# Column sums from chunks that GpSimd added before, and a correction whose two parts share one matmul

## The chip, the cores and the metric

The kernel runs on one core of one Trainium2 chip. Its engines work at the same time and meet through semaphores: TensorE (PE) for matmuls, with its weight loads shown apart as PEld, VectorE (DVE), ScalarE (ACT), GpSimd (POOL), and SyncE (SP), which issues the DMAs. The metric is the device time of one execution in microseconds (us), median of several runs.

## The reference, cut to what matters

A decoder layer for 2 x 256 tokens of width 512: self-attention with 32 heads, then a product with a context in fake-quantised numbers, then a linear layer with low-rank experts. The change touches the second of the three.

```python
def fake_quant(x, scale, zp):
    s = scale.reshape(()); z = zp.reshape(())
    q = jnp.clip(jnp.round(x / s + z), 0.0, 255.0)
    return (q - z) * s

def _L0_xattn_ref(x1, x2, x1_scale, x1_zp, x2_scale, x2_zp):
    return jnp.matmul(fake_quant(x1, x1_scale, x1_zp), fake_quant(x2, x2_scale, x2_zp))

x = x + attn(layernorm(x), Wq, bq, Wk, bk, Wv, bv, Wo, bo, gq, gk)
x = x + _L0_xattn_ref(layernorm(x), ctx_4096, ...)     # ctx: (2, 512, 512)
x = x + ffn(layernorm(x), ...)
```

## The kernel before, in words

The 512 tokens are four tiles of 128 partitions (t = 0 to 3, two for each batch). Projections, scores and products of the attention are done in float32 split into a high and a low part (`_hi`, `_lo`, three matmuls for each product); ScalarE makes the high part, VectorE or GpSimd subtracts it to make the low part.

**Order of the work.** Every engine has its own list of instructions, written out by hand, and executes it in that order; semaphores hold it where it needs another engine. First all heads of K and Q are projected. Then come 16 pairs of heads (`pair(p)`, p = 0 to 14, and `last_pair`). A pair has four slots (j = 0 to 3), one for each head and batch. In a slot TensorE does the scores of the *next* slot (L602 to L604), the transposes of the normalised probabilities (L611), a quarter of the V projection of the next pair (L625 to L627), the output projection of the previous head (L639 to L641) and probabilities times V (L670 to L672).

**GpSimd in a pair** (L1086): in slots 0 and 2 it makes the low parts of k and q for the next head (`split_kq_lo`, L1070 and L1072), then the low part of a piece of the V weights (`w_lo`, L1062); in slots 1 and 3 the low part of the output weights (`wo_lo`, L1062). TensorE waits for k_lo and q_lo (semaphore `kq_lo`) before the scores in slots 1 and 3. SP waits for GpSimd's weight parts (`w_lo_pool`) before it loads the next weights into the same place.

**VectorE in a slot**: maximum of the scores (`nmax`, L1293), its product with the row scale (`nbias`, L1295), which ScalarE needs for the exponentials (L858), the low part of the probabilities (L1368), and, after the exponentials, the reciprocal of the sum (L1300) and the two halves of the normalisation (L1302 and L1303), which TensorE needs for the transposes (semaphore `p_normed`).

**The quantised product.** Codes of context and activations are kept with 128 taken off, as small whole numbers. So the product of real values needs two corrections: one for each row (made later, `row_sums`), and one for each column, the sum of the context's codes down its 512 rows times a constant. The context is quantised early, waits in HBM as bf16 and comes back as `ctx_q` (4 chunks of 128 rows for each batch) at 413 us. For each batch `column_sums` multiplies a matrix of ones with the four chunks (L421), ScalarE scales the sums into `corr_hi` (L880), VectorE makes the remainder `corr_lo` (L1431), and `add_column_part` adds both to each token tile in `acc[t]` by multiplying with the identity (L429, L430). `column_sums(0)` stands in slot 3 of the last pair, `column_sums(1)` behind it, `add_column_part` behind the attention.

Of the kernel before, what the change touches and what calls it, by code (L numbers as in the profile page):

```python
# [19 lines left out]
F32 = mybir.dt.float32  # L20
F32R = mybir.dt.float32r
BF16 = mybir.dt.bfloat16
I32 = mybir.dt.int32
ALU = mybir.AluOpType
ACT = mybir.ActivationFunctionType
AX = mybir.AxisListType

P = 128
B, S, D = 2, 256, 512
T = B * S  # L30
NT = T // P
NC = D // P
SKV = 512
NH, DH = 32, 128
NP = NH // 2
# [14 lines left out]
def decoder_layer(nc, x, ctx_t, wk, wq, wv, wo, bk, bq, bv, bo, gk, gq, qscal, ra_w, base_b, router_b, bm_w,  # L50
                  expert_map, out):
    st = ExitStack()
    with st:
        def sem(name):
            return st.enter_context(nc.semaphore(name))
# [18 lines left out]
        def here(name, shape, dt, at=None):  # L74
            return place(name, shape, dt, at)[0]
# [4 lines left out]
        q_all, q_at = place("q_all", [P, NH, T], F32)  # L80
# [17 lines left out]
        ident_r = here("ident_r", [P, P], F32R)  # L98
# [19 lines left out]
        qc = here("qc", [P, 8], F32)  # L118
# [3 lines left out]
        half = NT * PW * 4  # L122
# [8 lines left out]
        KS = T * 4  # L131
# [20 lines left out]
        ctx_q = here("ctx_q", [P, B * NC, SKV], BF16, k_at + 18 * KS)  # L152
        xn = here("xn", [P, NT, D], F32, q_at)
        q1t = here("q1t", [P, NT, NC, P], BF16, q_at + 6 * KS)
        corr_hi = here("corr_hi", [P, B, SKV], F32R, q_at + 8 * KS)
        corr_lo = here("corr_lo", [P, B, SKV], F32R, q_at + 4 * KS)
        hw = here("hw", [P, NT, P], F32, q_at + 10 * KS)
        ones_b = here("ones_b", [P, P], BF16, q_at + 11 * KS)
        small_at = q_at + 12 * KS
        emf = here("emf", [P, NR], F32, small_at)  # L160
        onehot = here("onehot", [P, NE, NR], F32, small_at + 128)
# [26 lines left out]
        acc = [bank(f"acc{t}", [P, D]) for t in range(NT)]  # L188
# [4 lines left out]
        p_flat = [p_v[:].rearrange("p a b -> p (a b)"), p_s[:].rearrange("p a b -> p (a b)"),  # L193
                  p_t[:].rearrange("p a b -> p (a b)"), p_o[:]]
# [50 lines left out]
        ctx_back = sem("ctx_back")  # L245
# [15 lines left out]
        wo_last_done = sem("wo_last_done")  # L261
        x1_ready = sem("x1_ready")
        ones_b_made = sem("ones_b_made")
        ctx_quantised = sem("ctx_quantised")
        col_sums_ready = sem("col_sums_ready")
        col_part_done = sem("col_part_done")
# [41 lines left out]
        def peeled(n, first, end):  # L308

            return isinstance(n, int) and first <= n < end  # L310
# [104 lines left out]
        def column_sums(pe, b):  # L415

            if b == 0:
                pe.wait_ge(ctx_back, 16)
                pe.wait_ge(ones_b_made, 1)
            for c in range(NC):  # L420
                mm = pe.matmul(p_flat[b], ones_b[:], ctx_q[:, b * NC + c, :], start=(c == 0), stop=(c == NC - 1))  # L421
            mm.then_inc(col_sums_ready, 1)

        def add_column_part(pe, t):

            if t % 2 == 0:
                pe.wait_ge(col_lo_done, t // 2 + 1)
            pe.wait_ge(linear_done, t + 1)
            pe.matmul(acc[t][:], ident_r[:], corr_hi[:, t // 2, :], start=False, stop=False, skip_group_check=True)  # L429
            pe.matmul(acc[t][:], ident_r[:], corr_lo[:, t // 2, :], start=False, stop=True, skip_group_check=True  # L430
                      ).then_inc(col_part_added, 1)

        def transpose_q1(pe, t):
# [341 lines left out]
        def _(act):  # L775
# [101 lines left out]
            def column_part(b):  # L877

                act.wait_ge(col_sums_ready, b + 1)
                act.activation(corr_hi[:, b, :], p_flat[b], ACT.Copy, scale=qc[:, 3:4]  # L880
                               ).then_inc(col_part_done, 1)

            def last_out_hi(n):
# [140 lines left out]
        def _(pool):  # L1024
# [52 lines left out]
            def mark_experts():  # L1077
# [5 lines left out]
                    ins = pool.tensor_scalar(onehot[:, e, :], emf[:], float(e), None, ALU.is_equal)  # L1083
                ins.then_inc(experts_marked, 1)

            def pair(p, par):  # L1086
                for j in range(4):
                    h = 2 * p + j // 2
                    if j % 2 == 0:
                        split_kq_lo(h + 1)  # L1090
                        pair_chunk_lo(par, j // 2, 0, 4 + 4 * p + j)
                    else:
                        chunk_lo(wo_lo[:], wo_hi[:], 1, 4 + 4 * p + j)
                    if peeled(p, NP - 5, NP - 4) and j == 0:
                        pool.memset(ones_b[:], 1.0).then_inc(ones_b_made, 1)

            def last_pair():
                n = 4 + 4 * (NP - 1)
# [28 lines left out]
        def _(dve):  # L1127
# [79 lines left out]
            for r in range(1, 4):  # L1207
# [4 lines left out]
                                          op0=ALU.mult, op1=ALU.mult))  # L1212
# [215 lines left out]
            def column_lo(b):  # L1428

                dve.wait_ge(col_part_done, b + 1)  # L1430
                dve.scalar_tensor_tensor(out=corr_lo[:, b, :], in0=p_flat[b], scalar=qc[:, 3:4],  # L1431
                                         in1=corr_hi[:, b, :], op0=ALU.mult, op1=ALU.subtract
                                         ).then_inc(col_lo_done, 1)

            def row_part():
# [101 lines left out]
            for t in range(NT):  # L1537
# [5 lines left out]
                                          op0=ALU.is_lt, op1=ALU.mult))  # L1543
# [6 lines left out]
            for t in range(NT):  # L1550

                ins = dve.scalar_tensor_tensor(out=hw[:, t, :].rearrange("p (e r) -> p e r", e=NE),
                                               in0=acc[t][:, 0:P].rearrange("p (e r) -> p e r", e=NE), scalar=2.0,
                                               in1=gate[:, t, :].unsqueeze(2).to_broadcast([P, NE, RK]),
                                               op0=ALU.mult, op1=ALU.mult)
# [4 lines left out]
            for n, (t, cols, y) in enumerate(out_parts()):  # L1560
# [3 lines left out]
                                         in1=x_res[:, t, cols], op0=ALU.add, op1=ALU.add).then_inc(out_done, 1)  # L1564
# [54 lines left out]
```

## Time and profile before

| | us |
|---|---|
| median of 3 runs (533.52 to 533.87) | 533.6 |
| span of the profiled execution, first to last instruction | 531.9 |
| what lies around the span (533.6 less 531.9; the profiled execution's own time is not listed apart) | 1.7 |
| TensorE busy, share of the span | 520.5, 98% |
| VectorE busy | 332.6, 63% |
| ScalarE busy | 354.6, 67% |
| GpSimd busy | 264.4, 50% |

The granted TensorE clock is 1.000 over the span, the higher of its two levels (2.4 GHz). Matmuls are pipelined and their ends are modelled, so for TensorE the step from one start to the next counts, not the duration of one. The times in the rows further down are microseconds from the span's start. In that count the attention's pairs run from about 194 to 492 us, a pair takes 18.8 us and a slot 4.7 us.

### The profile page before, as it was taken

How to read it: one execution, taken by the hardware profiler on the slowest of the kernel's cores; microseconds unless marked ns; L12 is line 12 of the kernel's file. 1: busy time of each engine (PE TensorE's matmuls, PEld its weight loads, DVE VectorE, ACT ScalarE, POOL GpSimd, SP SyncE). 2: the span in 40 equal slices, each digit the busy share in tenths (PEclk: the TensorE clock that was granted, in tenths of full speed). 3: DMA queues.
4: the chain of work that ended last, by engine and by line, in shares of the span. 5: the costliest groups of instructions: out<-in, count | busy, mean ns of one | idle time of the engine just before them, and what ended most of it. 6: DMA issues, size and time to landing. Idle time of an engine off the chain costs nothing.

```text
span 531.9 us, 9795 instructions
## 1 busy us (share of the span) xinstructions
PE 520.5 (98%) x3221; PEld 462.3 (87%) x3221; DVE 332.6 (63%) x703; ACT 354.6 (67%) x743; POOL 264.4 (50%) x223
## 2 busy tenths in 40 slices
PE   7999999999999999999999999999999999999897
PEld 6888888878888888999999999999999999997586
DVE  6354444276666677666766666666666677766855
ACT  4666665656666767767767776777767777766730
POOL 2444444364455545564646556465564646542340
PEclk9999999999999999999999999999999999999999
DMA  5445635323333221122121122211132322121002
GB/s 184 139 139 166 209 99 163 95 79 99 99 99 95 63 82 51 51 59 60 59 59 52 47 59 59 59 59 55 46 124 77 138 61 60 42 58 41 1 1 80
DMA packets 23495, 43.43 MB, mean 82 GB/s; under 512 B 3632, under 2 KB 3888, under 8 KB 23216
## 3 DMA queue, kind: packets, MB, share of 16 engines
q1 hardware_dynamic: 23472, 43.13, 27.0%
q8 instruction: 13, 0.21, 0.2%
q14 instruction: 10, 0.08, 0.1%
HBM read 41.03 MB, written 2.10 MB: 81 GB/s over the span
## 4 chain that ended last, share of the span: by engine, by line
PE 90%; DVE 5%; ACT 2%; DMA 1%; POOL 1%; issue 0%; SPq 0%; DVEq 0%; ACTq 0%
PE p_v L627 5%; PE p_v L625 5%; PE p_o L548 5%; PE p_o L549 5%; PE p_o L550 5%; PE p_v L626 5%; PE p_t L548 5%; PE p_t L550 5%; PE p_t L549 5%; PE acc L639 5%; PE acc L640 5%; PE p_t L611 5%; PE acc L641 5%; PE p_o L670 3%; PE p_o L672 3%; PE p_o L671 3%
## 5 line engine op out<-in xcount | busy, mean ns | idle before, releaser
L1193 DVE TENSOR_TENSOR w_lo<-raw,w_hi 128x512 fp32r<-128x512 f32 x64 | 44.2, 690 | 77.0 <-ACT w_hi L782 77.0
L1062 POOL TENSOR_TENSOR wo_lo<-raw,wo_hi 128x512 fp32r<-128x512 f32 x31 | 40.2, 1297 | 100.7 <-ACT wo_hi L936 97.2
L858 ACT ACTIVATE probs<-p_s,nbias,rq_t 128x256 f32<-128x256 f32 x128 | 71.3, 562 | 19.4 <-DVE nbias L1295 19.4
L782 ACT CAST w_hi<-raw 128x512 fp32r<-128x512 f32 x64 | 39.9, 623 | 62.7 <-PE p_t L550 30.3
L625 PE MATMUL p_v<-w_hi,xnt_hi 128*128 128x256 f32 x256 | 77.2, 302 | 0.0
L627 PE MATMUL p_v<-w_hi,xnt_lo 128*128 128x256 f32 x256 | 72.3, 283 | 0.0
L626 PE MATMUL p_v<-w_lo,xnt_hi 128*128 128x256 f32 x256 | 72.2, 282 | 0.0
L1044 POOL TENSOR_TENSOR acc_k<-acc_k,square 128x512 f32<-128x512 f32 x32 | 41.6, 1301 | 52.7 <-ACT square L797 52.7
L1044 POOL TENSOR_TENSOR acc_q<-acc_q,square 128x512 f32<-128x512 f32 x32 | 43.5, 1360 | 40.2 <-ACT square L797 39.9
L912 ACT CAST pt_hi<-p_t 128x512 fp32r<-128x512 f32 x64 | 37.4, 584 | 37.6 <-PE p_t L611 37.6
L1062 POOL TENSOR_TENSOR w_lo<-raw,w_hi 128x512 fp32r<-128x512 f32 x32 | 44.8, 1400 | 23.4 <-ACT w_hi L842 23.4
L1293 DVE TENSOR_REDUCE nmax<-p_s 128x2 f32<-128x512 f32 x64 | 43.9, 686 | 13.4 <-PE p_s L604 12.5
L548 PE MATMUL p_o<-xnt_hi,w_hi 128*128 128x512 f32 x128 | 49.8, 389 | 0.0
L549 PE MATMUL p_o<-xnt_hi,w_lo 128*128 128x512 f32 x128 | 49.8, 389 | 0.0
L550 PE MATMUL p_o<-xnt_lo,w_hi 128*128 128x512 f32 x128 | 49.8, 389 | 0.0
L625 PEld LDWEIGHTS p_v<-w_hi,xnt_hi 128*128 128x128 f32 x256 | 48.8, 191 | 0.3 <-issue 0.2
L626 PEld LDWEIGHTS p_v<-w_lo,xnt_hi 128*128 128x128 f32 x256 | 48.9, 191 | 0.0
L548 PE MATMUL p_t<-xnt_hi,w_hi 128*128 128x512 f32 x124 | 48.8, 393 | 0.0
L627 PEld LDWEIGHTS p_v<-w_hi,xnt_lo 128*128 128x128 f32 x256 | 48.7, 190 | 0.0
L550 PE MATMUL p_t<-xnt_lo,w_hi 128*128 128x512 f32 x124 | 48.3, 389 | 0.0
L549 PE MATMUL p_t<-xnt_hi,w_lo 128*128 128x512 f32 x124 | 48.3, 389 | 0.0
L639 PE MATMUL acc<-wo_hi,o_hi 128*128 128x512 f32 x120 | 47.6, 397 | 0.1
(287 smaller groups left out, 1486.7 us busy)
## 6 DMA issues: line engine op xcount, KB each, us to landing
raw<-in_wv SPq DMA_DIRECT2D x36, 256.0 KB, 2.6
raw<-in_wk SPq DMA_DIRECT2D x32, 256.0 KB, 2.6
raw<-in_wq SPq DMA_DIRECT2D x32, 256.0 KB, 2.6
raw<-in_wo SPq DMA_DIRECT2D x31, 256.0 KB, 2.6
ctx_f<-in_ctx SPq DMA_DIRECT2D x4, 512.0 KB, 3.7
xin<-in_x SPq DMA_DIRECT2D x4, 256.0 KB, 3.4
xb<-in_x SPq DMA_DIRECT2D x4, 256.0 KB, 5.6
ctx_kept<-ctx_k SPq DMA_DIRECT2D x1, 1024.0 KB, 5.0
```

Of the source, the lines that this page charges most:

```text
L548: pe.matmul(p_flat[2 + n], hi[:, c, :], xnt_hi[:, c, :], start=(c == 0), stop=False)
L549: pe.matmul(p_flat[2 + n], lo[:, c, :], xnt_hi[:, c, :], start=False, stop=False)
L550: mm = pe.matmul(p_flat[2 + n], hi[:, c, :], xnt_lo[:, c, :], start=False, stop=(c == NC - 1))
L625: pe.matmul(p_v[:, t % 2, :], xnt_hi[:, c, tt], hi[:, c, :], start=(c == 0), stop=False)
L626: pe.matmul(p_v[:, t % 2, :], xnt_hi[:, c, tt], lo[:, c, :], start=False, stop=False)
L627: mm = pe.matmul(p_v[:, t % 2, :], xnt_lo[:, c, tt], hi[:, c, :], start=False, stop=(c == NC - 1))
L639: pe.matmul(acc[t][:], o_hi[:, tt], wo_hi[:], start=False, stop=False, skip_group_check=True)
L858: act.activation(probs[:, n, a, :], p_s[:, a, :], ACT.Exp, bias=nbias[:, n, a:a + 1], scale=rq_t[:, 2 * b + a:2 * b + a + 1], accum_out=rs ...
L1044: pool.tensor_tensor(sums[:], sums[:], square[:, r % 2, :], ALU.add).then_inc(summed, 1)
L1062: pool.tensor_tensor(dst, raw[:, slot, :], hi, ALU.subtract).then_inc(w_lo_pool, 1)
L1193: dve.tensor_tensor(w_lo[:, n, 0:NC * DH], raw[:, r, :], w_hi[:, n, 0:NC * DH], ALU.subtract).then_inc(w_lo_dve, 1)
L1293: dve.tensor_reduce(nmax[:, n, :], p_s[:], AX.X, ALU.max, negate=True).then_inc(max_done, 1)
```

## The change

GpSimd adds the four chunks of each batch's context codes, with three additions of 128x512 for each batch, in slots 1, 2 and 3 of the pairs 13 and 14 (`add_ctx`). The sum is float32 (`ctx_sum`), and `column_sums` is one matmul for each batch in place of four. The correction's high part is written to all 128 partitions of `corr`, and VectorE then overwrites partitions 64 to 127 with the low part. All rows of each half are alike, so a matrix `two_rows` with ones in rows 0 and 64 and zeros elsewhere adds one row of each: one matmul for each token tile in place of two. GpSimd makes the new constants in pair 11.

```diff
-        corr_hi = here("corr_hi", [P, B, SKV], F32R, q_at + 8 * KS)
-        corr_lo = here("corr_lo", [P, B, SKV], F32R, q_at + 4 * KS)
+        ctx_sum = here("ctx_sum", [P, B, SKV], F32R, q_at + 8 * KS)
+        corr = here("corr", [P, B, SKV], F32R, q_at + 4 * KS)
...
+        ones_r = here("ones_r", [P, P], F32R, q_at + 11 * KS + 512)
+        two_rows = here("two_rows", [P, P], F32R, q_at + 11 * KS + 1024)
...
         def column_sums(pe, b):
             if b == 0:
-                pe.wait_ge(ctx_back, 16)
-                pe.wait_ge(ones_b_made, 1)
-            for c in range(NC):
-                mm = pe.matmul(p_flat[b], ones_b[:], ctx_q[:, b * NC + c, :], start=(c == 0), stop=(c == NC - 1))
-            mm.then_inc(col_sums_ready, 1)
+                pe.wait_ge(ones_b_made, 4)
+            pe.wait_ge(ctx_summed, (NC - 1) * (b + 1))
+            pe.matmul(p_flat[b], ones_r[:], ctx_sum[:, b, :], start=True, stop=True).then_inc(col_sums_ready, 1)
...
             pe.wait_ge(linear_done, t + 1)
-            pe.matmul(acc[t][:], ident_r[:], corr_hi[:, t // 2, :], start=False, stop=False, skip_group_check=True)
-            pe.matmul(acc[t][:], ident_r[:], corr_lo[:, t // 2, :], start=False, stop=True, skip_group_check=True
+            pe.matmul(acc[t][:], two_rows[:], corr[:, t // 2, :], start=False, stop=True, skip_group_check=True
                       ).then_inc(col_part_added, 1)
...
-                act.activation(corr_hi[:, b, :], p_flat[b], ACT.Copy, scale=qc[:, 3:4]
+                act.activation(corr[:, b, :], p_flat[b], ACT.Copy, scale=qc[:, 3:4]
                                ).then_inc(col_part_done, 1)
...
+            def add_ctx(b, c):
+                if c == 1:
+                    pool.wait_ge(ctx_back, 16)
+                    first = ctx_q[:, b * NC, :]
+                else:
+                    pool.wait_ge(ctx_summed, (NC - 1) * b + c - 1)
+                    first = ctx_sum[:, b, :]
+                pool.tensor_tensor(ctx_sum[:, b, :], first, ctx_q[:, b * NC + c, :], ALU.add).then_inc(ctx_summed, 1)
+
             def pair(p, par):
                 for j in range(4):
...
                     if peeled(p, NP - 5, NP - 4) and j == 0:
                         pool.memset(ones_b[:], 1.0).then_inc(ones_b_made, 1)
+                        pool.memset(ones_r[:].bitcast(F32), 1.0).then_inc(ones_b_made, 1)
+                        pool.memset(two_rows[:].bitcast(F32), 0.0).then_inc(rows_cleared, 1)
+                        pool.wait_ge(rows_cleared, 1)
+                        pool.memset(two_rows[0:1, :].bitcast(F32), 1.0).then_inc(ones_b_made, 1)
+                        pool.wait_ge(ones_b_made, 3)
+                        pool.memset(two_rows[P // 2:P // 2 + 1, :].bitcast(F32), 1.0).then_inc(ones_b_made, 1)
+                        pool.wait_ge(ones_b_made, 4)
+                    if peeled(p, NP - 3, NP - 1) and j > 0:
+                        add_ctx(p - (NP - 3), j)
...
-                dve.scalar_tensor_tensor(out=corr_lo[:, b, :], in0=p_flat[b], scalar=qc[:, 3:4],
-                                         in1=corr_hi[:, b, :], op0=ALU.mult, op1=ALU.subtract
+                half = slice(P // 2, P)
+                dve.scalar_tensor_tensor(out=corr[half, b, :], in0=p_flat[b][half], scalar=qc[half, 3:4],
+                                         in1=corr[half, b, :], op0=ALU.mult, op1=ALU.subtract
                                          ).then_inc(col_lo_done, 1)
```

GpSimd's list in the kernel before, from slot 1 of pair 13 to slot 1 of pair 14. `kq_hi` and `w_hi_done` are ScalarE's semaphores for high parts.

```order
L1062 TENSOR_TENSOR wo_lo<-raw,wo_hi 128x512 [waits w_hi_done]
L1070 TENSOR_TENSOR k_lo<-k_all,k_hi 128x512 [waits kq_hi]
L1072 TENSOR_TENSOR q_lo<-q_all,q_hi 128x512 [waits kq_hi]
L1062 TENSOR_TENSOR w_lo<-raw,w_hi 128x512 [waits w_hi_done]
L1062 TENSOR_TENSOR wo_lo<-raw,wo_hi 128x512 [waits w_hi_done]
L1070 TENSOR_TENSOR k_lo<-k_all,k_hi 128x512 [waits kq_hi]
L1072 TENSOR_TENSOR q_lo<-q_all,q_hi 128x512 [waits kq_hi]
L1062 TENSOR_TENSOR w_lo<-raw,w_hi 128x512 [waits w_hi_done]
L1062 TENSOR_TENSOR wo_lo<-raw,wo_hi 128x512 [waits w_hi_done]
```

The same stretch in the changed kernel; L1095 is the new addition.

```order
L1063 TENSOR_TENSOR wo_lo<-raw,wo_hi 128x512 [waits w_hi_done]
L1095 TENSOR_TENSOR ctx_sum<-ctx_q 128x512 [waits ctx_back]
L1071 TENSOR_TENSOR k_lo<-k_all,k_hi 128x512 [waits kq_hi]
L1073 TENSOR_TENSOR q_lo<-q_all,q_hi 128x512 [waits kq_hi]
L1063 TENSOR_TENSOR w_lo<-raw,w_hi 128x512 [waits w_hi_done]
L1095 TENSOR_TENSOR ctx_sum<-ctx_sum,ctx_q 128x512 [waits ctx_summed]
L1063 TENSOR_TENSOR wo_lo<-raw,wo_hi 128x512 [waits w_hi_done]
L1095 TENSOR_TENSOR ctx_sum<-ctx_sum,ctx_q 128x512 [waits ctx_summed]
L1071 TENSOR_TENSOR k_lo<-k_all,k_hi 128x512 [waits kq_hi]
L1073 TENSOR_TENSOR q_lo<-q_all,q_hi 128x512 [waits kq_hi]
L1063 TENSOR_TENSOR w_lo<-raw,w_hi 128x512 [waits w_hi_done]
L1063 TENSOR_TENSOR wo_lo<-raw,wo_hi 128x512 [waits w_hi_done]
```

Nothing of the old list has changed its order, but the additions of slots 1 and 3 stand in front of k_lo and q_lo, and that of slot 2 stands between w_lo and wo_lo. Pair 14 has the same three, and the last of them has no k_lo behind it, since head 31 is split elsewhere.

TensorE's list in the kernel before, from the last slot of the attention to the first correction. `q1_done` is VectorE's semaphore for quantised activations, `linear_done` ScalarE's for the step ahead of it.

```order
L421 MATMUL p_s<-ctx_q,ones_b 128x512 x4
L657 MATMUL acc<-wo_last_hi,o_last_hi 128x512 [waits wo_last_done,o_lo_done]
L658 MATMUL acc<-wo_last_hi,o_last_lo 128x512
L659 MATMUL acc<-wo_last_lo,o_last_hi 128x512
L657 MATMUL acc<-wo_last_hi,o_last_hi 128x512
L658 MATMUL acc<-wo_last_hi,o_last_lo 128x512
L659 MATMUL acc<-wo_last_lo,o_last_hi 128x512
L439 MATMUL p_t<-ident,xn 128x128 [waits q1_done]
L439 MATMUL p_t<-ident,xn 128x128 x3
L429 MATMUL acc<-corr_hi,ident_r 128x512 [waits linear_done,col_lo_done]
L430 MATMUL acc<-corr_lo,ident_r 128x512
L429 MATMUL acc<-corr_hi,ident_r 128x512 [waits linear_done]
```

And in the changed kernel:

```order
L424 MATMUL p_s<-ctx_sum,ones_r 128x512 [waits ctx_summed]
L658 MATMUL acc<-wo_last_hi,o_last_hi 128x512 [waits wo_last_done,o_lo_done]
L659 MATMUL acc<-wo_last_hi,o_last_lo 128x512
L660 MATMUL acc<-wo_last_lo,o_last_hi 128x512
L658 MATMUL acc<-wo_last_hi,o_last_hi 128x512
L659 MATMUL acc<-wo_last_hi,o_last_lo 128x512
L660 MATMUL acc<-wo_last_lo,o_last_hi 128x512
L440 MATMUL p_t<-ident,xn 128x128 [waits q1_done]
L440 MATMUL p_t<-ident,xn 128x128 x3
L431 MATMUL acc<-corr,two_rows 128x512 [waits linear_done,col_lo_done]
L431 MATMUL acc<-corr,two_rows 128x512 [waits linear_done]
```

Six matmuls of the column sums and four of the correction are gone; the rest keeps its order, and so do VectorE's and ScalarE's lists.

## Rows read from the trace of the kernel before

**Rows 1.** The page, part 4: shares of the chain that ended last.

```profile
PE 90%; DVE 5%; ACT 2%; DMA 1%; POOL 1%; issue 0%; SPq 0%; DVEq 0%; ACTq 0%
```

**Rows 2.** Busy time by stretch: the stretch, its length, each engine's busy time.

```profile
448.48:457.87 9.39, 9.39 (x71) 8.85 (x70) 6.75 (x16) 7.12 (x18) 5.29 (x4) 1.00 0.20 56
```

**Rows 3.** GpSimd in order of time: start, length, operation, idle before and releaser.

```profile
448.84 1.33 POOL L1062 TENSOR_TENSOR wo_lo<-raw,wo_hi 128x512 fp32r<-128x512 f32 x1 [3.25 <-ACT wo_hi L936]
450.45 1.30 POOL L1070 TENSOR_TENSOR k_lo<-k_all,k_hi 128x512 fp32r<-128x512 f32 x1 [0.29 <-ACT k_hi L845]
451.71 1.29 POOL L1072 TENSOR_TENSOR q_lo<-q_all,q_hi 128x512 fp32r<-128x512 f32 x1
453.59 1.42 POOL L1062 TENSOR_TENSOR w_lo<-raw,w_hi 128x512 fp32r<-128x512 f32 x1 [0.59 <-ACT w_hi L842]
...
458.23 1.33 POOL L1062 TENSOR_TENSOR wo_lo<-raw,wo_hi 128x512 fp32r<-128x512 f32 x1 [3.22 <-ACT wo_hi L936]
...
461.10 1.30 POOL L1072 TENSOR_TENSOR q_lo<-q_all,q_hi 128x512 fp32r<-128x512 f32 x1
...
467.62 1.32 POOL L1062 TENSOR_TENSOR wo_lo<-raw,wo_hi 128x512 fp32r<-128x512 f32 x1 [3.23 <-ACT wo_hi L936]
...
470.25 1.30 POOL L1072 TENSOR_TENSOR q_lo<-q_all,q_hi 128x512 fp32r<-128x512 f32 x1
```

**Rows 4.** TensorE's weight loads in order of time: first scores of slots, a transpose.

```profile
453.18 0.19 PEld L602 LDWEIGHTS p_s<-k_hi,q_hi 128*128 128x128 f32 x1
...
453.92 0.14 PEld L611 LDWEIGHTS p_t<-ident,probs 128*128 128x128 f32 x1
...
462.57 0.19 PEld L602 LDWEIGHTS p_s<-k_hi,q_hi 128*128 128x128 f32 x1
...
471.95 0.19 PEld L602 LDWEIGHTS p_s<-k_hi,q_hi 128*128 128x128 f32 x1
```

**Rows 5.** VectorE in order of time, slot 2 of pair 13.

```profile
451.28 0.49 DVE L1295 TENSOR_TENSOR nbias<-nmax,rq_t 128x2 f32<-128x2 f32 x1
...
453.24 0.36 DVE L1302 TENSOR_SCALAR probs<-probs,rinv 128x256 f32<-128x256 f32 x1
453.51 0.35 DVE L1303 TENSOR_SCALAR probs<-probs,rinv 128x256 f32<-128x256 f32 x1
```

**Rows 6.** VectorE and GpSimd in order of time, where they meet at 113 us.

```profile
112.96 0.69 DVE L1193 TENSOR_TENSOR w_lo<-raw,w_hi 128x512 fp32r<-128x512 f32 x1
...
113.24 1.56 POOL L1044 TENSOR_TENSOR acc_q<-acc_q,square 128x512 f32<-128x512 f32 x1 [1.12 <-ACT square L797]
...
113.57 1.78 DVE L1198 SCALAR_TENSOR_TENSOR k_all<-k_all,g_c,rkb 128x512 f32<-128x512 f32 x1
```

**Rows 7.** The chain that ended last, in order of time: start, length, work.

```profile
475.62 0.24 PE acc L641
...
477.95 2.79 DMA raw<-in_wo
...
490.75 0.86 PE p_v L421 x4
...
497.56 0.23 PE acc L430
```

**Rows 8.** VectorE, ScalarE and TensorE in order of time, behind the attention.

```profile
493.09 0.74 DVE L1431 SCALAR_TENSOR_TENSOR corr_lo<-p_v,qc,corr_hi 128x512 fp32r<-128x512 f32 x1
494.26 0.48 DVE L1344 SCALAR_TENSOR_TENSOR o_last_lo<-p_o,bv_c,o_last_hi 128x256 fp32r<-128x256 f32 x1 [0.42 <-ACT o_last_hi L888]
...
497.36 0.69 ACT L983 ACTIVATE q1t<-p_t,qc 128x512 bf16<-128x512 f32 x1 [0.54 <-PE p_t L439]
...
498.11 0.39 PE L450 MATMUL p_v<-ctx_q,q1t 128*128 128x512 bf16 x1
...
502.61 0.42 DVE L1419 TENSOR_SCALAR xn<-xn 128x512 f32<-128x512 f32 x1
...
503.08 0.65 PE L439 MATMUL p_o<-ident,xn 128*128 128x128 f32 x4
```

More of the change, by code:

```diff
@@ L263, in decoder_layer @@
         ones_b_made = sem("ones_b_made")
+        rows_cleared = sem("rows_cleared")
+        ctx_summed = sem("ctx_summed")
         ctx_quantised = sem("ctx_quantised")
```

## The prediction

> **What bounds the kernel now.** I read the page first. Its chain of the work that ended last lies on TensorE for 90% [rows 1]: a stall of TensorE costs its own length unless something slower runs beside it. Then the busy times by stretch: two slots of pair 13 and 14, 9.39 us, are filled by TensorE without a gap, GpSimd is busy for 5.29 us of them [rows 2]. So GpSimd has 4.1 us free in two slots, but the average does not say where. The engine's own rows do [rows 3]: its free time lies in front of wo_lo (3.25 us) and in front of w_lo (0.59 us); wo_lo, k_lo and q_lo follow each other with hardly a gap (448.84, 450.45, 451.71). q_lo ends at 451.71 + 1.29 = 453.00, and the scores that wait for it start on TensorE at 453.18 [rows 4]. These 0.18 us are the number on which the forecast rests. Last I read the chain in order of time around 475 us and behind the attention [rows 7], and VectorE's rows there [rows 8].
>
> **What the change removes.** Ten matmuls of 128x512. The four bf16 ones of a column sum take 0.86 us on the chain, 0.215 each; a correction matmul takes 0.23 [rows 7]. That is 6 x 0.215 + 4 x 0.23 = 2.2 us of TensorE time at most, if all of it were on the path. The one that stays of each four now has fp32r inputs; the correction's own matmuls have them too and take 0.23, so I price it at that.
> The Trainium skill (FP8 and Floating Point Precision, TensorE Precision Notes) has true FP32 matmuls make four passes through the array, while its reduced-precision reading does not. Were the four-pass rule the one for this matmul, the column sums would save nothing; the 0.23 us of the row is one pass, so the trace sides with the reduced reading.
>
> How much of the 2.2 us is on the path:
> - Column sum 0 is in front of the last output projections. Its three matmuls, 0.65 us, let the last p_o end earlier. But o_last_lo, which follows p_o, stands on VectorE behind corr_lo, which does not move: it ends at 493.09 + 0.74 = 493.83, and o_last_lo started at 494.26 [rows 8]. With the next instruction following about 0.07 us before the end of the one ahead, o_last_lo comes at 493.78: 0.5 us gained, the rest lost in this wait. Everything up to the first quantised tile hangs on it.
> - Column sum 1 runs while TensorE would wait for o_last_lo anyway: 0. It only lets ScalarE's column part come early enough for the 0.5 to pass on.
> - Corrections of tiles 0 and 1: the product behind them needs q1t, which ends at 497.36 + 0.69 = 498.05; it started at 498.11 [rows 8]. 0 to 0.06, I take 0.
> - Corrections of tiles 2 and 3: the transposes behind them started at 503.08, 0.05 after VectorE's quantisation ended at 502.61 + 0.42 = 503.03 [rows 8]. 0.
> VectorE's remainder on half the partitions has as many elements in each partition; I give it the old 0.74. Gain in all: 0.5 us. Bounds: 0, and the 2.2 us.
>
> **What it adds: first stall, the scores.** No row shows GpSimd adding bf16. The nearest are its 128x512 fp32 instructions with two inputs: 1.29 to 1.56 us long [rows 3, 6], and 451.71 - 450.45 = 1.26 from start to start. I take 1.28 and, as bounds, 0.5 (no row is near it) and 1.6. Three of the six additions stand in front of k_lo and q_lo:
> - Pair 13, slot 1. wo_lo starts at 448.84, so the addition at 450.12, k_lo at 451.40 in place of 450.45, and q_lo ends at 453.95 in place of 453.00. The scores start on TensorE about 0.06 behind it, at 454.01 in place of 453.18: 0.83 us.
> - Pair 13, slot 3. wo_lo 458.23, addition 459.51, k_lo 460.77, q_lo 462.03 to 463.33 in place of 461.10 to 462.40; scores 463.39 in place of 462.57: 0.82.
> - Pair 14, slot 1. wo_lo 467.62, addition 468.90, k_lo 470.16, q_lo 471.42 to 472.72; scores 472.78 in place of 471.95: 0.83. Here 0.40 us lay between the old q_lo and the scores, but GpSimd had no gap to give.
> Together 2.5 us. In a formula each is the addition's time less 0.45.
>
> **Second stall, the normalisation.** The same late q_lo covers VectorE's normalisation. In the rows nbias, a 128x2 product of two tiles in SBUF, takes 0.49 us from 451.28, to 451.77, just behind the end of k_lo at 451.75 [rows 3, 5]: VectorE was held until GpSimd's instruction ended. The halves of the normalisation (453.24 and 453.51) escaped this, because q_lo was over at 453.00 and w_lo came at 453.59, and its 1.42 us instead of 1.29 say that w_lo waited for the second half instead. Now: nbias waits for the addition only (to 451.47), the exponentials and with them the first half come 0.3 earlier, at 452.93, but q_lo runs from 452.66 to 453.95. The first half gets in at its end. w_lo, whose high part is ready, stands right behind. At 113.24 a GpSimd instruction was waiting when VectorE's at 112.96 ended, and the next of VectorE, at 113.57, took 1.78 us: the waiting GpSimd instruction went first [rows 6]. By this the second half waits for w_lo, which ends at 453.90 + 1.38 = 455.3, and is done at 455.4. The transposes, which started at 453.92 [rows 4], start at 455.45: 1.53 us late, 0.83 of it already counted. So 0.7 us more; the other two places, with the same distances, give 0.7 each. Together 2.1 us. Bounds: 0 (the second half slips in before w_lo) and 1.0 each (the first half is held too).
> The Trainium skill (SBUF — State Buffer, Who interferes with whom) says that VectorE's two-port modes and GpSimd exclude each other for a whole instruction, and that the order of issue decides who waits. By issue order w_lo (453.90) is ahead of the second half (454.02), which gives the same 0.7; but this margin of 0.1 us is what makes the second stall less sure than the first.
>
> **What stays at nothing.** The additions behind w_lo (slot 2) lie in the 3.2 us in front of wo_lo [rows 3]; 1.28 us fit even with w_lo 1.7 late, as TensorE's own delay moves wo_lo by 1.5. They may hold one nbias, inside that same delay. The last addition (pair 14, slot 3) comes behind the last wo_lo that starts the 2.79 us weight transfer on the chain [rows 7], and can hold VectorE only beside it: 0, at most 0.2. If that cover were gone it would cost one addition. SP's weight loads wait for w_lo, 1.7 late, but the copy of those weights comes two slots later. The memsets in pair 11 fall into the same kind of 3.2 us gap. The new wait of TensorE for the sums is over 10 us old when it gets there.
>
> **Does a stall come back?** The chain leaves TensorE at 475.62, with the output projection that frees wo_hi, and goes on over wo_lo and the transfer [rows 7]. All three places are earlier, and TensorE has no idle time between them and there that could be used up. So all of it counts.
>
> **Sum.** +2.5 + 2.1 - 0.5 = +4.1 us on the profiled 531.9 us of span, 536.0; with the 1.7 us around the span 537.7, which is also the median 533.6 + 4.1.
>
> **The rivals.**
> 1. *Only the scores stall.* The second half of the normalisation slips in. For it: the margin of 0.1 us, and that no normalisation in the trace was ever held. Against it: 113 us. 533.6 + 2.5 - 0.5 = 535.6. If it slips in at some of the three places, 536.3 or 537.0.
> 2. *A longer addition.* The bf16 input or the mixed types cost GpSimd more, 1.6 us: three times 0.3 more, 538.6. Nothing in the trace speaks for or against.
> 3. *Faster: the additions are short.* If two bytes an element make them cheap, the stalls of 3 x (a - 0.45) fall under the gain of 0.5 once an addition a takes less than 0.62 us, and the normalisation is then not covered. At 0.45 us or less the time is 533.6 - 0.5 = 533.1. Against it: every GpSimd instruction with 512 elements and two inputs in the rows takes twice that.
> 4. *No change.* Stalls of the scores for a short addition of 0.6 us against the gain: 533.6.
>
> **Chances.** Forecast 50%, the first rival with its mixed cases 31%, the second 9%, the third 5%, the fourth 5%. About 0.2%, 1.1 us, is what a measurement of this kernel can tell from no change. Faster 0.04, same 0.06, slower 0.90. The range takes in the first two rivals and the bounds around them and leaves out the third and fourth: 534.8 to 539.0.
>
> **What will show it.** Right: the scores' first weight load in slots 1 and 3 shows idle time of 0.7 to 0.9 us released by GpSimd's q_lo, three times, and nowhere else; L1303's longest row grows from 0.35 to over 1 us three times, and the transposes wait for it; behind the attention the first quantised tile comes 0.5 us sooner relative to the end of the last slot. The first step is wrong if GpSimd's additions last under 0.6 us or TensorE shows no idle there. The second is wrong if L1303 stays at 0.35. The gain is wrong if the stretch from the last transposes of the attention to the end shrinks by more than 0.7 us or not at all.

## The result

| | before | after |
|---|---|---|
| median, same chip (4 runs each) | 533.72 | 536.53 (536.49 to 536.88) |
| span of the profiled execution | 531.9 | 535.0 |

The ratio is 1.0053 (95% interval 1.0039 to 1.0066): the change costs 2.8 us. The forecast was 4.1 (537.7), the range 534.8 to 539.0. The direction held. The two stalls of the forecast came together at one of its three places; at the other two a third one, which it did not name, stood instead. That the range holds 536.5 is in part luck.

I set the weight loads of both traces side by side, instruction by instruction, and noted where the distance grows. It is 0.52 us after the first microseconds (the input's transposes, before anything that changed; the profiled run is the longest of its four), stays so for 440 us, and then:

| place, time after | distance | TensorE waits for |
|---|---|---|
| pair 13 slot 1, 453.7 | 0.52 to 1.28 | pt_lo |
| pair 13 slot 3, 463.9 | 1.28 to 2.02 | pt_lo |
| pair 14 slot 1, 474.6 and 476.1 | 2.02 to 3.38 | q_lo, then probs |
| pair 14 slot 3, 483.1 | to 3.54 | |
| weight transfer, 486.5 | to 3.15 | |
| column sums, 494.0 | to 2.54 | |
| o_last_lo, and up to 506.1 | 2.90, 3.07 | |

Three places cost 0.76 + 0.74 + 1.36 = 2.86 us. The last addition (pair 14 slot 3) costs 0.16 us more, beside the weight transfer. Behind the attention 0.5 to 0.6 us is won (3.15 to 2.54) and nearly all lost again (3.07 at the end). Some 0.2 of the step at the transfer belongs to the profiled run of before: the kernel of e13_waits_only below, with the work of before, shows 0.2 there too. The other 0.2 is about what the last addition had cost.

### The profile page after: what moved, and what is told of

It is laid out like the page before. It is cut to its first block, busy times and chain, and to the rows that moved or that the text cites. A ratio compares the mean times of both kernels' runs of the same rounds, so it can differ in the third digit from the quotient of the medians.

```text
span 535.0 us, 9785 instructions
## 1 busy us (share of the span) xinstructions
PE 520.3 (97%) x3210; PEld 461.7 (86%) x3211; DVE 336.2 (63%) x703; ACT 354.3 (66%) x743; POOL 271.5 (51%) x233
## 4 chain that ended last, share of the span: by engine, by line
PE 86%; DVE 7%; ACT 3%; DMA 1%; POOL 1%; issue 1%; SPq 0%; DVEq 0%; ACTq 0%
PE p_o L549 5%; PE p_o L551 5%; PE p_o L550 5%; PE p_t L549 5%; PE p_t L551 5%; PE p_t L550 5%; PE p_v L626 5%; PE p_v L628 5%; PE p_v L627 5%; PE acc L640 5%; PE acc L641 5%; PE p_t L612 5%; PE acc L642 5%; PE p_o L671 3%; PE p_o L673 3%; PE p_o L672 2%
```

## The profile after

The page, part 4, answers to [rows 1]; TensorE's share is 4% lower than before:

```profile
PE 86%; DVE 7%; ACT 3%; DMA 1%; POOL 1%; issue 1%; SPq 0%; DVEq 0%; ACTq 0%
```

The third place first, since there both stalls of the forecast are seen. GpSimd, VectorE and TensorE's weight loads in order of time, pair 14 slot 1; they answer to [rows 3, 4]:

```profile
469.64 1.32 POOL L1063 TENSOR_TENSOR wo_lo<-raw,wo_hi 128x512 fp32r<-128x512 f32 x1 [3.24 <-ACT wo_hi L937]
470.93 1.16 POOL L1095 TENSOR_TENSOR ctx_sum<-ctx_q 128x512 fp32r<-128x512 bf16 x1
472.05 1.28 POOL L1071 TENSOR_TENSOR k_lo<-k_all,k_hi 128x512 fp32r<-128x512 f32 x1
473.31 1.27 POOL L1073 TENSOR_TENSOR q_lo<-q_all,q_hi 128x512 fp32r<-128x512 f32 x1
474.55 1.32 POOL L1063 TENSOR_TENSOR w_lo<-raw,w_hi 128x512 fp32r<-128x512 f32 x1
...
471.71 0.40 DVE L1315 TENSOR_TENSOR nbias<-nmax,rq_t 128x2 f32<-128x2 f32 x1
...
473.58 1.15 DVE L1322 TENSOR_SCALAR probs<-probs,rinv 128x256 f32<-128x256 f32 x1
474.65 1.36 DVE L1323 TENSOR_SCALAR probs<-probs,rinv 128x256 f32<-128x256 f32 x1
...
474.63 0.19 PEld L603 LDWEIGHTS p_s<-k_hi,q_hi 128*128 128x128 f32 x1 [0.58 <-POOL q_lo L1073]
...
476.07 0.20 PEld L612 LDWEIGHTS p_t<-ident,probs 128*128 128x128 f32 x2 [0.66 <-DVE probs L1323]
```

The scores wait for q_lo. The two halves of the normalisation, 0.35 us of work each, take 1.15 and 1.36: the first is held until q_lo ends (474.58), and w_lo, which starts there, goes ahead of the second.

The first place went another way. The same engines, pair 13 slot 1; nbias and probs answer to [rows 5]:

```profile
449.36 1.31 POOL L1063 TENSOR_TENSOR wo_lo<-raw,wo_hi 128x512 fp32r<-128x512 f32 x1 [3.23 <-ACT wo_hi L937]
450.62 1.16 POOL L1095 TENSOR_TENSOR ctx_sum<-ctx_q 128x512 fp32r<-128x512 bf16 x1
451.75 1.29 POOL L1071 TENSOR_TENSOR k_lo<-k_all,k_hi 128x512 fp32r<-128x512 f32 x1
453.00 1.27 POOL L1073 TENSOR_TENSOR q_lo<-q_all,q_hi 128x512 fp32r<-128x512 f32 x1
...
451.80 1.25 DVE L1315 TENSOR_TENSOR nbias<-nmax,rq_t 128x2 f32<-128x2 f32 x1
452.98 0.68 DVE L1388 TENSOR_TENSOR pt_lo<-p_t,pt_hi 128x512 fp32r<-128x512 f32 x1
...
454.52 0.35 DVE L1322 TENSOR_SCALAR probs<-probs,rinv 128x256 f32<-128x256 f32 x1
454.79 0.35 DVE L1323 TENSOR_SCALAR probs<-probs,rinv 128x256 f32<-128x256 f32 x1
...
453.71 0.19 PEld L671 LDWEIGHTS p_o<-pt_hi,v_hi 128*128 128x128 f32 x1 [0.88 <-DVE pt_lo L1388]
...
454.41 0.19 PEld L603 LDWEIGHTS p_s<-k_hi,q_hi 128*128 128x128 f32 x1
```

The addition ends at 450.62 + 1.16 = 451.78 and k_lo starts at 451.75. nbias, 0.16 us of work when free, starts at 451.80, 0.05 behind k_lo, and is held until k_lo ends at 453.04. VectorE works in order, so pt_lo is late and TensorE waits for it, 0.88 us (0.76 of it new), ahead of the scores. That wait hides the late q_lo (454.27, scores 454.41), and the exponentials come so late that the normalisation meets no q_lo. At the second place the same: k_lo 461.87, nbias 461.90 and 1.28 long.

Behind the attention, VectorE in order of time, against [rows 8]. The first row is of before, the others of the changed kernel (`vare` is the variance that the layer norm needs next):

```profile
493.02 0.17 DVE L1405 TENSOR_SCALAR vare<-mv 128x2 f32<-128x2 f32 x1
...
496.17 0.17 DVE L1425 TENSOR_SCALAR vare<-mv 128x2 f32<-128x2 f32 x1
496.37 0.76 DVE L1452 SCALAR_TENSOR_TENSOR corr<-p_v,qc,corr 64x512 fp32r<-64x512 f32 x1
497.16 0.48 DVE L1364 SCALAR_TENSOR_TENSOR o_last_lo<-p_o,bv_c,o_last_hi 128x256 fp32r<-128x256 f32 x1
```

corr starts 0.20 after vare's start, where corr_lo stood 0.07 after it in the trace of before, and o_last_lo starts only when corr has ended (497.13), not 0.07 ahead of its end.

## The experiments

**e1_adds_only.** The kernel before with the six additions (`add_ctx`) where the changed kernel has them, and nothing else of the change; the sums go unused.

```
+        ctx_sum = here("ctx_sum", [P, B, SKV], F32R, q_at)
...
+                    if peeled(p, NP - 3, NP - 1) and j > 0:
+                        add_ctx(p - (NP - 3), j)
```

> The kernel before with the six GpSimd additions in their new places, and nothing else of the change: column sums and corrections stay as before, the additions' result is not used. Theory (the additions alone make the kernel slower, through places 1 to 3 in front of k_lo and q_lo): the same three stalls of TensorE as in the changed kernel, 0.8, 0.75 and 1.35 us, 0.2 of it won back at the weight transfer, so +2.7 us, 536.4. Rival (part of the 2.8 us comes from the new matmuls or the new wait for the sums): clearly under +2.7, 535.5 or less.

Measured: 536.55 us (536.31 to 536.73), before 533.86, ratio 1.0052 (1.0039 to 1.0066). The loss comes from the additions. The changed kernel lost 2.8 us on its before and this one 2.7, so the matmuls that fell away gave nothing that these runs can tell. nbias was 1.28, 1.26 and 0.39 us long at the three places, as in the changed kernel.

**e4_longer.** The two additions ahead of k_lo in pair 13 take 576 columns instead of 512 (the 64 more land where the second batch's sums are written later). They last 1.30 us.

```
+                if b == 0 and c != 2:
+                    n = SKV + 64
...
+                    pool.tensor_tensor(sums[:, 0:n], first, flat[:, c * SKV:c * SKV + n], ALU.add)
```

> The changed kernel with the two additions of pair 13 that stand in front of k_lo 64 columns longer, 576 in place of 512 (the surplus is overwritten later). Theory (what is lost hangs on which GpSimd instruction nbias meets): the additions last 0.13 us longer, 1.29 in place of 1.16, end behind the moment nbias is issued, and nbias slips in at their end, in place of missing it by 0.02 us and waiting out k_lo. Then these two places turn into what pair 14 shows, scores late by about 0.75 us and transposes by 0.65 more: +1.3 us, 537.8. Rival (each addition costs its length): 2 x 0.13 = +0.26 us, 536.8.

Measured: 538.15 us (537.3 to 538.46), ratio 1.0083 (1.007 to 1.0097). VectorE and TensorE at the first place:

```profile
450.94 0.16 DVE L1323 TENSOR_TENSOR nbias<-nmax,rq_t 128x2 f32<-128x2 f32 x1
...
452.57 1.15 DVE L1330 TENSOR_SCALAR probs<-probs,rinv 128x256 f32<-128x256 f32 x1
453.64 1.37 DVE L1331 TENSOR_SCALAR probs<-probs,rinv 128x256 f32<-128x256 f32 x1
...
453.63 0.19 PEld L603 LDWEIGHTS p_s<-k_hi,q_hi 128*128 128x128 f32 x1 [0.73 <-POOL q_lo L1073]
...
455.06 0.20 PEld L612 LDWEIGHTS p_t<-ident,probs 128*128 128x128 f32 x2 [0.67 <-DVE probs L1331]
```

0.14 us more on an addition moves k_lo past nbias, and both stalls of the forecast are there, 0.73 + 0.67 us; the second place shows the same two waits, 0.73 and 0.67. With additions of about the length that I had assumed (1.28) in pair 13, the loss is 4.3 us on this before (533.86), beside the 4.1 of the forecast. It is 0.35 more than I had expected of this run; its trace, of the shortest of the five runs, shows 1.4 us more at the three places than the changed kernel.

**e5_behind_q.** The three additions stand behind q_lo instead of ahead of k_lo.

> The changed kernel with the three additions that stood in front of k_lo now behind q_lo, in front of w_lo. Theory (the shared port alone costs): k_lo and q_lo are on time, but the addition holds the first half of the normalisation until it ends, w_lo goes ahead of the second half, and the transposes come 1.5 us late at three places: +4.5 us on the kernel before, 538.2. If w_lo does not go ahead of the second half: 0.5 us a place, 535.1. Rival (what costs is that k_lo and q_lo are late): nothing is late for TensorE, 533.6.

Measured: 538.22 us (537.9 to 538.6), ratio 1.0085 (1.0071 to 1.0098). Pair 13:

```profile
453.24 1.17 POOL L1095 TENSOR_TENSOR ctx_sum<-ctx_q 128x512 fp32r<-128x512 bf16 x1
454.36 1.31 POOL L1063 TENSOR_TENSOR w_lo<-raw,w_hi 128x512 fp32r<-128x512 f32 x1
...
453.51 1.04 DVE L1328 TENSOR_SCALAR probs<-probs,rinv 128x256 f32<-128x256 f32 x1
454.48 1.35 DVE L1329 TENSOR_SCALAR probs<-probs,rinv 128x256 f32<-128x256 f32 x1
...
455.88 0.20 PEld L612 LDWEIGHTS p_t<-ident,probs 128*128 128x128 f32 x2 [1.64 <-DVE probs L1329]
```

No score waits here; the held normalisation alone makes TensorE wait 1.6, 1.6 and 1.4 us at the three places. So holding the normalisation costs by itself, without a late k_lo or q_lo. The first half is held by the addition, the second by w_lo: one GpSimd instruction each.

**e2_gaps.** The additions stand behind w_lo, in slots 0 and 2 of pairs 12 to 14, where GpSimd is idle for 3.2 us.

```
-                    if peeled(p, NP - 3, NP - 1) and j > 0:
-                        add_ctx(p - (NP - 3), j)
+                    if peeled(p, NP - 4, NP - 1) and j % 2 == 0:
+                        n = 2 * (p - (NP - 4)) + j // 2
+                        add_ctx(n // 3, n % 3 + 1)
```

> The changed kernel with each addition behind w_lo, in slots 0 and 2 of pairs 12, 13 and 14, where GpSimd has 3.2 us free, none in front of k_lo. Theory (only the place of the additions costs): no stall of TensorE at scores, probabilities or transposes; the tail keeps its gain of 0.1 to 0.26 us; 533.5, that is 0.2 us under the kernel before and 3.0 under the changed one. Rival (GpSimd's additions cost wherever they stand, through the port that VectorE shares with it): six additions cost about 0.4 us each, 536.

Measured: 535.02 us (533.69 to 536.44, 7 runs), before 533.86, ratio 1.0024 (1.0011 to 1.0037): neither value. Its trace has one new cause of stalls, in pair 13 (0.5 us of TensorE, then 1.0):

```profile
445.70 1.16 POOL L1095 TENSOR_TENSOR ctx_sum<-ctx_sum,ctx_q 128x512 fp32r<-128x512 f32 x1
...
445.70 1.18 DVE L1316 TENSOR_TENSOR nbias<-nmax,rq_t 128x2 f32<-128x2 f32 x1
...
449.48 1.55 DVE L1379 TENSOR_TENSOR bm_lo<-bm_f,bm_hi 128x512 fp32r<-128x512 f32 x1
...
452.32 1.12 DVE L1316 TENSOR_TENSOR nbias<-nmax,rq_t 128x2 f32<-128x2 f32 x1
...
454.10 0.19 PEld L671 LDWEIGHTS p_o<-pt_hi,v_hi 128*128 128x128 f32 x1 [1.12 <-DVE pt_lo L1389]
```

nbias and the addition start in the same moment and nbias is held. That makes VectorE 1 us late, its next instruction with two SBUF inputs (bm_lo) meets wo_lo, and the next nbias meets q_lo. At 426.90 and 465.97 the two also started together, and there nbias lasted 0.16. A coin, it seemed, which would explain a spread of 2.7 us over 7 runs. A later nbias (475.35, 0.96 long, 0.23 behind the start of an addition) is held too and costs TensorE nothing.

**e6_low_first, e8_gated, e9_gated_low.** The first is the changed kernel with the low part on partitions 0 to 63. The others are e2_gaps with a gate meant to settle the coin, and with both edits.

```
 e6, e9:
-                half = slice(P // 2, P)
+                half = slice(0, P // 2)
 e8, e9, ahead of add_ctx:
+                        pool.wait_ge(nb_done, 4 * p + j + 2)
```

> The changed kernel with one slice turned round: VectorE writes the low part on partitions 0 to 63 instead of 64 to 127 (the high part then stands on 64 to 127; the sum over the two rows is the same). In the changed kernel corr lasts 0.76 us and begins 0.20 after vare, and o_last_lo begins only when it ends. Theory: VectorE's instructions on the upper half wait for the pipeline on either side, about 0.12 us twice. Then on the lower half corr begins 0.07 after vare, o_last_lo 0.07 before corr's end, and the matmul part of the gain is whole: 0.2 to 0.25 us less than the changed kernel, 536.3 beside its 536.5. Rival: the two gaps come from the semaphore wait on ScalarE's corr or from reading p_flat and corr with fewer partitions; then nothing moves, 536.5.

> The whole change, with the six additions behind w_lo in slots 0 and 2 of pairs 12 to 14, and ahead of each a wait of GpSimd for that slot's nbias. In the run with the additions in those slots and no such wait, nbias and the addition started at the same moment three times; nbias was held once (445.70, 1.18 us, the ungated run cost 1.2 us over the kernel before), and not at 426.90 (0.16). Theory: the only cost in these slots is that coincidence, and an addition that starts after nbias ends before the two scalings of probs 1.4 us later. Then no nbias and no probs is held in these slots, TensorE has no new idle time up to the tail, and the tail's gain of 0.26 stands alone: 533.6 beside a kernel before of 533.86 (533.4 to 533.8). Rival A: the additions still hold the scalings of probs or late_lo (bm_lo), 534.5 or more. Rival B: GpSimd's shared access slows others in a way that no held instruction shows, and the additions cost 0.1 to 0.2 each wherever they stand: 534.5.

> The additions waiting for nbias in slots 0 and 2 of pairs 12 to 14, and the low part on partitions 0 to 63: both corrections at once. By both theories the tail's gain is 0.45 to 0.5 us and nothing else is lost: 533.4 beside a kernel before of 533.86, ratio 0.999, the only version expected to beat the kernel before. Rival: the gain in the tail is taken back by GpSimd's later work there (onehot and rstd end later in the changed kernel by 0.15 us), 533.6, no difference that can be told.

Measured: e6 536.0 us (535.89 to 536.91), ratio 1.0042 (1.0029 to 1.0055); e8 534.24 (533.88 to 535.95, 12 runs), 1.0015 (1.0005 to 1.0025); e9 535.08 (533.06 to 536.85, 12 runs), 1.0019 (1.0004 to 1.0033); before 533.78.

In e6 the tail behaves as on full partitions again:

```profile
496.65 0.17 DVE L1425 TENSOR_SCALAR vare<-mv 128x2 f32<-128x2 f32 x1
496.73 0.73 DVE L1452 SCALAR_TENSOR_TENSOR corr<-p_v,qc,corr 64x512 fp32r<-64x512 f32 x1
497.39 0.47 DVE L1364 SCALAR_TENSOR_TENSOR o_last_lo<-p_o,bv_c,o_last_hi 128x256 fp32r<-128x256 f32 x1
```

The distance to before falls by 0.51 us at the column sums and stays there to the last transposes. The medians are 0.5 apart (536.53 and 536.0, each on its own chip; as losses on their own before 2.8 and 2.2, with intervals that overlap), twice what I expected. In the trace of the changed kernel the gain since the transfer is 0.25 us behind o_last_lo (3.15 to 2.90) and 0.08 from 506.1 on; here it is 0.5 in both places. The gaps beside corr account for the first difference; what makes the second was not tested. There the last of eight `onehot` of GpSimd lasts 0.52 us in place of 0.25 (all eight 2.45 us against 2.19 here). The firmer comparison is e10 against e11 below: the same chip, 11 runs each, only the half exchanged, 534.29 and 533.89. The Trainium skill (VectorE: DVE Perf Modes, Two Vector instructions with no wait between them) says that an instruction whose operands start in another group of 32 partitions than those before it is held until all earlier ones end, and so is the next one that changes back. The trace agrees: 0.20 and 0.79 us from start to start on the upper half, 0.08 and 0.66 on the lower. My rival, that the semaphore or the smaller number of partitions makes the gaps, falls with it: both are the same on the lower half.

The gate was one slot too early: `nb_done` stands one higher beside these additions than I had counted, and the wait was long over. So in e8 and e9 the additions start beside nbias as in e2_gaps, and the coin is thrown again. The first two rows are of e8, the last two of e9, in the same place:

```profile
464.37 0.16 DVE L1317 TENSOR_TENSOR nbias<-nmax,rq_t 128x2 f32<-128x2 f32 x1
...
464.38 1.18 POOL L1095 TENSOR_TENSOR ctx_sum<-ctx_sum,ctx_q 128x512 fp32r<-128x512 f32 x1
```

```profile
464.31 1.19 DVE L1317 TENSOR_TENSOR nbias<-nmax,rq_t 128x2 f32<-128x2 f32 x1
...
464.31 1.16 POOL L1095 TENSOR_TENSOR ctx_sum<-ctx_sum,ctx_q 128x512 fp32r<-128x512 f32 x1
```

With the same order of both lists the stall is there once and once not. In e9 it costs TensorE 1.1 us in the slot behind it (L671 at 472.71 waits 1.13 for pt_lo) and 0.5 ahead of that. Over the traces of e2, e8 and e9, an nbias that starts 0.01 us or more ahead of the addition is free; at less than 0.01 us between them both outcomes occur (0.16 at 426.90 and 465.97, 1.18 at 445.70, 1.19 at 464.31), and the recorded starts do not say which it will be.

**e10_gate_next, e11_gate_next_low.** The gate one count further, `4 * p + j + 3`; e11 with the low part below.

> In e8_gated the wait named the nbias of the slot before and gated nothing: nbias 426.80 and the addition 426.81, 445.59 and 445.60, 464.37 and 464.38 still start together, and its runs spread from 533.88 to 535.95. Here the wait is for the next count of nb_done, the nbias that stands beside the addition. Theory: whichever of the two instructions asks first takes the access, so such a pair is a coin that falls anew in each execution; with the wait every nbias lasts 0.16, each addition starts 0.1 to 0.2 after it and ends before the scalings of probs, the runs lie within 0.6 us of each other, and the median is 533.5 (before less the tail's 0.26). Rival: the spread has another cause (start of the execution, transfers); then the runs spread by 2 us again and the median stays at 534.2.

> The same wait, and the low part on partitions 0 to 63. In e6_low_first the matmul part of the gain was 0.51 us and stayed to the end. Theory: runs close together, median 533.3 beside a kernel before of 533.8 (0.5 less). Rival: as for e10_gate_next, a spread of 2 to 3 us and a median of 534 to 535, as in e9_gated_low (533.06 to 536.85).

Measured: e10 534.29 us (534.03 to 534.5, 11 runs), ratio 1.0009 (1.0 to 1.0018); e11 533.89 (533.48 to 534.28, 11 runs), 1.0003 (0.9994 to 1.0012); before 533.64. The spread fell to 0.5 and 0.8 us, beside 1.1 for before on this chip (1.9 on the chip of e8 and e9): the coin is gone, as the theory said. The medians are 0.8 and 0.6 above what I expected. In the traces no instruction is held that was not held before, and the additions add nothing to TensorE's distance to before. About half of the missing time lies outside the span: the medians of time less span are 1.85 to 1.90 us for before, 1.82 to 1.91 for the kernels up to e6, and 2.33, 2.32, 2.30 and 2.21 for e8 to e11. The other half lies inside, with median spans of 532.0 and 531.7 beside 531.7, where 0.26 and 0.5 less were due. In the profiled runs it stands in the first 13 us, which nothing of the change touches: TensorE is 0.35 and 0.38 us later there than in the profiled run of before, and wins 0.3 and 0.7 from there to the end. This start lies between 0.34 earlier (e4) and 0.86 later (e6) in the traces here, and what moves it stays open. Those four (e8 to e11) have GpSimd's program six instructions longer than the changed kernel's (200 against 194).

**e12_fewer, e13_waits_only.** e12 is e11 with six GpSimd instructions less: `two_rows` becomes a full matrix of 1/64, made by one memset (each half's 64 equal rows, summed), the column sum uses ones that are there anyway, and two waits of GpSimd go, the gate of the last addition among them; e13 is before with 17 more (34 waits, packed in pairs).

```
 e12:
-                        pool.memset(ones_r[:].bitcast(F32), 1.0).then_inc(ones_b_made, 1)
...
+                        pool.memset(two_rows[:].bitcast(F32), 2.0 / P).then_inc(ones_b_made, 1)
...
-                        pool.wait_ge(nb_done, 4 * p + j + 3)
+                        if n < 5:
+                            pool.wait_ge(nb_done, 4 * p + j + 3)
 e13:
+                        for _ in range(34):
+                            pool.wait_ge(made, 5)
```

> e11_gate_next_low with GpSimd's program six instructions shorter, 194 instead of 200 (as many as in the changed kernel): the two-row matrix is a full one of 1/64 (64 equal rows of corr in each half, summed), its four memsets and their waits are one; the column sum takes the ones that are there from the start; the last addition has no gate and the second batch's first no wait for ctx_back. In the runs with 194 the execution's time stood 1.87 to 1.91 us over the span, in the four with 200 it stood 2.21 to 2.33. Theory: the length of GpSimd's program decides that step; then it is 1.9 again, and with the tail's 0.5 and no held nbias the median is 533.45 beside a kernel before of 533.7, ratio 0.9993 to 0.9997. Rival: the waits for nb_done make it, whatever the length; then 2.3 and 533.9.

> The kernel before, with 34 waits of GpSimd that are long fulfilled, in the idle stretch behind the memset of ones_b (17 instructions, so that its program has 200 instead of 183). Nothing else is changed and no engine waits for GpSimd there. Theory on the length: the time over the span rises from 1.88 to 2.3 us, the span stays, 534.1 beside 533.7. Rival: it stays 1.88, and the step of the gated kernels has another cause.

Measured: e12 533.17 us (532.69 to 534.12, 11 runs), before 533.78 (21 runs), ratio 0.999 (0.9981 to 0.9999); time less span 1.87. e13 534.5 us (533.98 to 535.48, 11 runs), ratio 1.0014 (1.0005 to 1.0023); time less span 2.30, its median span 532.2 beside 532.0. For the time outside the span both are as the theory on the length has it: e12 keeps five of the six gates and shows no step, e13 has no gate and shows it. It is the length of the program or something that goes with it (its place in memory, say); where between 194 and 200 the step lies, and what takes the 0.4 us, stays open, since no record lies outside the span. e12's median is also 0.3 below what I expected.

e12, and one gate of it in pair 13:

```profile
445.69 0.16 DVE L1313 TENSOR_TENSOR nbias<-nmax,rq_t 128x2 f32<-128x2 f32 x1
...
447.32 0.35 DVE L1320 TENSOR_SCALAR probs<-probs,rinv 128x256 f32<-128x256 f32 x1
447.59 0.35 DVE L1321 TENSOR_SCALAR probs<-probs,rinv 128x256 f32<-128x256 f32 x1
...
445.93 1.17 POOL L1096 TENSOR_TENSOR ctx_sum<-ctx_sum,ctx_q 128x512 fp32r<-128x512 f32 x1 [0.20 <-DVE nbias L1313]
```

The addition lies between nbias and the halves of the normalisation, 1.5 us in which VectorE runs only pt_lo, which reads PSUM, and the reciprocal. The last addition has no gate; it holds an nbias (473.84, 0.96 us), and TensorE loses nothing there. e12 drops the same ten matmuls as the change, and it is the only version faster than before: by 0.6 us, about what the column sums gave in the trace of e6_low_first. The interval ends at 0.9999, so this gain is just clear of the noise; how much of it is the start of the execution is not known.

## Why the prediction was right, and where it was off

- *What bounds the kernel*: right. TensorE's new waits add up to the loss, and of the three places nothing came back before the tail: of the 0.4 us at the transfer one half is the profiled run of before, the other about the 0.16 of the last addition, which the prediction had put beside the transfer at 0 to 0.2.
- *The addition's length*: mis-sized. 1.28 us taken, 1.16 to 1.21 measured, 1.13 from start to start. The formula "addition less 0.45" still holds where the scores wait: 1.13 - 0.45 = 0.68, measured 2.68 - 2.02 = 0.66 at the third place.
- *First and second stall, third place*: the mechanisms right, 0.66 + 0.70 us against 0.83 + 0.7, though the first half of the normalisation was held too (1.15 us). The order "second half behind w_lo" held there, and at all three places of e5_behind_q.
- *First and second place*: the step that failed is "Now: nbias waits for the addition only (to 451.47)". With 0.15 us less on the addition its end and the arrival of nbias fall together, k_lo goes first, and nbias is held through k_lo. The stall is then one, 0.76 and 0.74 us, not two of 1.5 together; a held instruction cost less than the two it took the place of. That is 1.5 of the 1.7 us between forecast and sum at the three places (4.6 against 2.86); e4_longer shows it by restoring the addition's length. The prediction had seen nbias held by k_lo in [rows 5] and still asked only what would hold it *less*. Its own figures have nbias come at 451.28 and k_lo at 451.40: a margin of 0.12 us, far less than the bounds of 0.5 and 1.6 that it gave the addition. So two of its signs were seen once and not three times: a first score that waits for q_lo (0.58 us, where 0.7 to 0.9 was given), and a second half of over 1 us.
- *The gain*: 0.5 us forecast, 0.1 left at the end. The rule "the next instruction follows 0.07 us before the end of the one ahead" was taken from instructions on all partitions; corr on the upper half does not obey it. On the lower half the 0.5 stayed to the end in the trace (e6_low_first), and e11 is 0.4 us shorter than e10. "I give it the old 0.74" held for the duration and missed the hand-over.
- *What stays at nothing*: right for the memsets and the additions behind w_lo, but by luck for slot 2 of pair 13. e2_gaps shows that this place can hold an nbias when both start together. In the changed kernel the slot behind is already 1 us late.
- *The rivals*: none came true. The first (only the scores stall) gives 535.6, and its case with one held normalisation 536.3, by another road: at two places it was not the scores that waited. The measured 536.5 lies inside the range because one unnamed stall of 0.75 us happened to cost about as much as the score stall alone (0.83) would have. That is luck, and the number alone confirms neither.

## What to carry to other kernels

- An addition on an idle engine is not free where that engine shares access with one on the path: look at which instructions of the other get longer beside it (here nbias, bm_lo and the halves of the normalisation, which read only SBUF; not pt_lo or nmax, which read PSUM) and place the work between them, held there by a semaphore, not by the time at which it happens to arrive. Two such instructions that start within 0.01 us of each other were a coin worth over 1 us, and a wider spread of the runs was its sign: 2.1 to 3.8 us, beside 1.1 to 1.9 for before and 0.5 to 1.4 with the gate.
- When a forecast rests on an order of two starts, compute it again for every duration within its bounds: 0.12 us on one addition changed which of two stalls appears and moved the sum by 1.6 us.
- Where one of two halves of the partitions goes to the engine on the path, give it the one at which its neighbouring instructions start, here the lower.

## What the hardware showed that I had not expected

- GpSimd's 128x512 addition takes 1.15 to 1.21 us, with two bf16 inputs or with one bf16 and one fp32r (shown as f32), against 1.27 to 1.32 for a difference of two 4-byte tiles in the rows of the changed kernel above.
- An nbias that starts 0.01 us or more ahead of GpSimd's instruction goes first (0.16 us), and VectorE gets in between two GpSimd instructions only if it stands ready when the first ends: 0.03 us late (461.90 against 461.87) and it lasts 1.28 us. One instruction of each then goes in turn (probs, w_lo, probs).
- Only some instructions of VectorE are held: beside k_lo and q_lo, pt_lo (452.98) takes its usual 0.68 us, and at the third place the halves of the normalisation, beside q_lo and w_lo, take 1.15 and 1.36 in place of 0.35.
- Time outside the span is not a constant of the chip: medians of 1.82 to 1.91 us with 183 to 194 instructions on GpSimd, 2.2 to 2.3 with 200; e13 does the work of before and has 2.30.
